# Second layer's attention: output products three tiles behind the scores instead of two

## The reference, cut to what matters

```python
def _L1_attn_ref(x, w_q_a, q_a_ln_w, w_q_b, w_kv_a, kv_a_ln_w, w_kv_b, w_o):
    ...
    q_full = jnp.concatenate([q_abs, q_pe], axis=-1)              # (b, s, 16, 128)
    k_full = jnp.concatenate([ckv, k_pe[:, :, 0, :]], axis=-1)    # (b, s, 128)
    scores = jnp.einsum('bqhd,bkd->bhqk', q_full, k_full) * sm_scale
    causal = jnp.tril(jnp.ones((s, s), dtype=bool))
    scores = jnp.where(causal[None, None], scores, jnp.finfo(scores.dtype).min)
    attn = jax.nn.softmax(scores, axis=-1)
    o_ckv = jnp.einsum('bhqk,bkr->bqhr', attn, ckv)
    y = jnp.einsum('bqhr,hre->bqe', o_ckv, w_o_abs)
    return y
```

## Time and profile before

| | us |
|---|---|
| median of 3 runs | 2657.73 |
| lowest and highest of them | 2649.23, 2659.24 |
| the profiled execution, whole | 2649.07 |
| its span, first to last instruction | 2647.1 |
| PE busy in the span | 2142.4 (81%) |
| ACT busy | 1163.7 (44%) |
| POOL busy | 699.5 (26%) |
| DVE busy | 1307.3 (49%) |

### The profile page before, as it was taken

One profiled execution on the slowest core, in us unless ns is written; L12 is line 12 of the kernel. 1 busy time (PEld: TensorE's weight loads), 2 busy tenths in 40 slices (PEclk: granted clock), 3 DMA queues, 4 the chain that ended last, 5 costly groups with the idle time before them and its releaser, 6 DMA issues. The chain is left out here.

```text
span 2647.1 us, 39558 instructions
## 1 busy us (share of the span) xinstructions
PE 2142.4 (81%) x10988; PEld 1373.2 (52%) x10988; DVE 1307.3 (49%) x2944; ACT 1163.7 (44%) x2316; POOL 699.5 (26%) x800
## 2 busy tenths in 40 slices
PE   5886899999872128999974579999978899997798
PEld 2542223333241114788864235777764577775587
DVE  5776778888127003344432566444425544442543
ACT  1663567777611001222211225777723477774222
POOL 1331000000010750000001663666620166663100
PEclk6786899999955557999987788999989899998899
DMA  7800000000101520777764320011000001102000
GB/s 221 254 1 1 1 0 0 0 0 0 36 1 30 180 78 8 214 224 223 225 178 125 88 81 15 21 30 30 21 25 0 3 21 30 29 22 76 0 17 16
DMA packets 186659, 167.16 MB, mean 63 GB/s; under 512 B 18787, under 2 KB 172949, under 8 KB 186326
## 3 DMA queue, kind: packets, MB, share of 16 engines
q1 hardware_dynamic: 175510, 139.42, 18.3%
q0 software_dynamic: 9696, 26.75, 3.1%
q10 hardware_dynamic: 1376, 0.02, 0.0%
HBM read 96.15 MB, written 61.60 MB: 60 GB/s over the span
## 5 line engine op out<-in xcount | busy, mean ns | idle before, releaser
L2404 POOL TENSOR_TENSOR w_rest<-work,w_head 128x512 fp32r<-128x512 f32 (+3 forms) x384 | 395.5, 1036 | 294.6 <-ACT w_head L2361 274.4
L725 DVE TENSOR_REDUCE half_max<-m_ps 128x1 f32<-128x512 f32 x512 | 319.5, 684 | 69.3 <-PE m_ps L645 67.8
L2266 DVE TENSOR_REDUCE piece_max<-m_ps 128x1 f32<-128x512 f32 (+3 forms) x384 | 201.6, 553 | 279.8 <-PE m_ps L2191 211.3
L782 ACT ACTIVATE weights<-s_ps 128x512 f32<-128x512 f32 x512 | 264.7, 606 | 69.9 <-PE s_ps L664 69.3
L2357 ACT ACTIVATE work<-s_ps 128x512 f32<-128x512 f32 (+3 forms) x384 | 187.9, 489 | 145.6 <-PE s_ps L2218 85.6
L645 PE MATMUL m_ps<-kT,qT 96*128 (+1 forms) x512 | 210.7, 413 | 13.8 <-ACT weights L782 5.5
L664 PE MATMUL s_ps<-qT,kT 99*128 (+1 forms) x512 | 193.9, 389 | 20.8 <-ACT weights L782 20.3
L2361 ACT ACTIVATE w_head<-work 128x512 fp32r<-128x512 f32 (+3 forms) x384 | 201.5, 525 | 12.2
L2227 PE MATMUL o_ps<-w_head,lat_head 128*128 128x512 f32 (+3 forms) x384 | 171.4, 446 | 15.3 <-POOL w_rest L2404 15.3
L974 PE MATMUL ex_up_ps<-rowsT,ex_wgv 128*128 128x256 f32 (+1 forms) x768 | 177.9, 382 | 2.3 <-DMA ex_wo<-in_L_ffn_wo_dram 1.4
L974 PEld LDWEIGHTS ex_up_ps<-rowsT,ex_wgv 128*128 128x128 f32 (+1 forms) x768 | 143.5, 187 | 25.6 <-DMA ex_wo<-in_L_ffn_wo_dram 1.8
(11 more groups left out here) (363 smaller groups left out, 4262.5 us busy)
## 6 DMA issues: line engine op xcount, KB each, us to landing
slots<-zero SPq DMA_DIRECT2D x8, 3456.0 KB, 27.4
rows<-slots SPq DMA_DIRECT2D x64, 256.0 KB, 2.8
slots<-ex_out SPq DMA_DIRECT2D x64, 256.0 KB, 2.1
ex_wgv<-in_L_ffn_wg_dram SPq DMA_DIRECT2D x76, 176.0 KB, 2.7
ex_wgv<-in_L_ffn_wv_dram SPq DMA_DIRECT2D x76, 176.0 KB, 3.2
ex_wo<-in_L_ffn_wo_dram SPq DMA_DIRECT2D x76, 128.0 KB, 3.1
oT<-work SPq DMA_DIRECT2D x64, 128.0 KB
w_down<-l_inverse SPq DMA_DIRECT2D x32, 256.0 KB, 3.8
```

What stands on the lines that cost most here:

```text
L725: dve.tensor_reduce(half_max[:, u // 16, u // 2 % 8, u % 2:u % 2 + 1], m_ps[:, BANK[u], :], AX.X, ALU.max).then_inc(max_done, 1)
L782: act.activation(w[:, s % 2 * 4 + j, :], s_ps[:, BANK[4 * s + j], :], ACT.Exp, scale=HD ** -0.5).then_inc(w_done, 1)
L2266: dve.tensor_reduce(piece_max[:, qt, k0 // 512:k0 // 512 + 1], m_ps[:, r % 2, 0:n], AX.X, ALU.max).then_inc(d["max_done"], 1)
L2404: pool.tensor_tensor(w_rest[:, s % 3, c0:512], w[:, s % 3, c0:512], w_head[:, s % 3, c0:512], ALU.subtract).then_inc(d["w_rest_done"], 1)
```

## The change

`LAG` goes from 2 to 3. PE issues the outputs of a tile behind the scores of the third tile after it; the outputs of tiles 9, 10 and 11 now come in the next head, or, for the last head, behind its last scores. DVE's two evacuations move one row maximum later, to stand again behind the outputs that they wait for. The buffers, their numbers and all waits on semaphores stay as they are.

```diff
-    LAG = 2
+    LAG = 3
...
-                        if behind and r == 3:
+                        if behind and r == 4:
                             evacuate(h - 1, 1)
-                        if r == 7:
+                        if r == 8:
                             evacuate(h, 0)
```

## The result

| | before | after |
|---|---|---|
| median, us | 2653.73 (6 runs) | 2627.76 (6 runs) |
| lowest and highest | 2648.61, 2659.24 | 2622.87, 2635.25 |
| profiled execution | 2649.07 | 2627.17 |
| its span | 2647.1 | 2625.2 |

The ratio is 0.9915 with a 95% interval of 0.9898 to 0.9933: the change makes the kernel 0.85% faster, some 22 us. Forecast were 19 us, and a time of 2638 in 2627 to 2650.

A forecast was written before the change was run, and what follows sets the result against it. PE was taken to bound the attention, waiting for w_rest at table loads. 12 x 1.25 = 15.0 us plus 4.0 in the last heads, seams zero, gave 19.0 off the median 2657.73: 2638 us, range 2627 to 2650.

The forecast's parts named there:

- What bounds the kernel: Second layer's attention: PE is the bound; twelve waits for POOL's w_rest ahead of a head's first outputs cost 1.25 us each.
- PE's arrival: At tile 0' outputs: PE arrives at 1711.49 after the change, against 1711.32 when the outputs could begin before.
- the chain on ACT: w_head of tile 11 waits for tile 8's outputs, ending 1706.43; it began at 1706.45 anyway, so timing holds within some 0.05 us.
- The forecast margin: At tile 0' outputs: w_rest is ready 0.12 to 0.17 us before PE arrives, so the whole wait goes.
- The cover: On ACT, place_shift (1.02 us) hides w_head of tile 11's new wait; without it the cost is up to 0.81 us.
- My slower rival: w_head holds back ACT's next exponential, so PE waits at tile 3' scores in every head; 2671 us; chance 0.04.
- DVE at nothing: DVE's evacuations (0.69 us each) move with their outputs; the row maximum behind has 1.3 us, so cost is nothing.
- The last heads: Each batch's last head: four waits, 0.67, 0.56, 0.24 and 0.22 us, go; worth 1.69 to 2.73, taken as 2.0, twice.
- Seams: Narrow blocks get other neighbours on PE: 0.09 us a seam, 2.9 us either way over 32 heads, taken as zero.
- The wait that is only shortened: Tile 8's outputs reach ACT's chain, 0.66 us of each of 12 waits stay; gain 11, 2647 us; chance 0.12.
- The collision of POOL and DVE: A 0.68 us query rest falls ahead of tile 0's w_rest; 0.53 us stay twelve times; 2645 us; chance 0.03.
- the change does nothing: The wait at a head's first outputs hangs on the free slot, not ACT; time stays 2657 us; chance 0.03.

The follow-up runs named there:

- without loads: Changed kernel (lag 3) with ACT's loop over pairs written out, so no table loads between heads: ratio 0.9915 to the kernel before, stretches 309.90 and 309.74 us.
- The padded kernel: Changed kernel (lag 3) plus one 512-column ACT copy into a spare tile behind every head's last tile: ratio 0.9949 to the kernel before.
- Lag 4: Changed kernel with LAG 4 instead of 3, same three slots, evacuations behind maxima 5 and 9: ratio 1.0048 to the kernel before, stretches 327.14 and 327.74 us.
- lag 2 without loads: Kernel before (lag 2) with ACT's loop over pairs written out, so no table loads between heads: ratio 0.9940, stretches 312.38 and 312.96 us.

## Why the prediction was right, point by point

**What bounds the kernel.** PE did, and each wait removed was time won. A loaded head fell from 20.51 to 19.26, by the 1.25 us that the periods had given, twelve times: 15.0 us as forecast (0.05 of the 1.25 is what the other heads gained too). A pair takes 38.47 us, where 38.5 was forecast.

**PE's arrival and the chain on ACT.** The sum put the outputs of tile 0' 11.49 - 4.57 = 6.92 us behind the turn of the maxima (1704.57). In the trace after they come 1707.30 - 1700.48 = 6.82 behind it. The forecast margin of 0.12 to 0.17 us was mis-sized: `w_rest` of tile 0' began at 1705.96 and takes 1.27, so it ended at 1707.23, 6.75 behind the turn. PE wanted it at almost the same moment: in heads without a load it reaches this block 6.79 us behind the turn. Two terms made the difference. On ACT, `w_head` of tile 11 began 0.05 us later behind the turn than before, as the sum had allowed, and everything behind it followed. On PE, the sum took 0.24 us from the row product to the outputs, but the outputs come 0.07 behind it where nothing holds them, here in the kernel before in a head without a load:

```profile
1690.68 0.39 PE L2188 MATMUL m_ps<-k_head,qT 128*128 128x512 bf16 x1
1690.75 0.56 PE L2227 MATMUL o_ps<-w_head,lat_head 128*128 128x512 f32 x1
```

That is 0.17 us less than the sum had; with 0.04 more in the other blocks PE is there at 6.79 and not 6.92, and the margin was no more than that. Loaded heads keep 0.05 us that the others don't (19.26 against 19.21, and 19.21 everywhere without loads). The padded kernel says the same, since its first 0.5 us are paid in full. That the 1.25 us went in full is luck in this sense: any 0.1 us more on ACT's chain would have come off the gain twelvefold.

**The cover.** That `place_shift` hides the new wait of `w_head` was right with lag 3: it began 1.93 us behind the turn (1702.41 less 1700.48) against 1.88 before. Lag 4 shows what the term is worth when the held `w_head` stands ahead of `place_shift`, not behind it: 1.0 us in every head. My slower rival had the kind right, ACT's queue held up by `w_head`, but named the exponential and tile 3' as the point where it decides. The `w_head` of tile 10, which stands ahead of `place_shift`, comes first, and I had not looked at it for lag 3 either.

**DVE at nothing.** Right, but only because the diff moves the evacuations as well; with the old places it is 0.8 us a head. At its old place the evacuation of tiles 0 to 3 holds up maximum 8, whose slot PE wants one block of scores behind the outputs that the evacuation waits for. At its new place it holds up maximum 9, whose slot PE wants another block of outputs and of scores later.

**The last heads.** 2.0 us each were forecast, and the last column shows 1.92, in the changed kernel and without loads. But the agreement is luck: with lag 3 PE has issued one 512-wide block of outputs less by the last maximum of each head, so that block is missing in the first head's time and is added to the last. It shows in the first head. From the row product behind the scores of its tile 2 to the next mark it takes 11.22 and 11.21 us before, 10.51 and 10.51 after. So the waits of a last head cost 1.92 + 0.70 = 2.6 us, near the upper end of the 1.69 to 2.73 and not the lower. The two short gaps cost a restart as well. Of the four waits one is left, on the last outputs:

```profile
1931.12 0.33 PE L2227 MATMUL o_ps<-w_head,lat_head 128*128 128x128 f32 x1 [0.16 <-POOL w_rest L2404]
```

**Seams.** Taken at zero within 2.9 us: the unloaded heads are 0.05 us shorter, some 0.7 us in both batches. The sign was open and the size is a quarter of the bound. That these are seams is not shown: no wait is listed in these heads with either lag, and the blocks' times differ by up to 0.1 us in both directions.

**The rest of the gain.** 15.0 from the loaded heads, 0.7 from the others and 5.2 from the last heads are 20.9 us, against the stretches' 20.65. What is left is the start of the first heads, behind a pause of PE, at a granted clock below full (0.59 in the 10 us from batch 1's first mark before, 0.62 after). From the first mark to that row product they take 7.19 and 8.12 us before and 7.73 and 7.92 after, 0.3 us more in all. This varies from run to run whatever the lag: 7.41 and 8.13 in the changed kernel again, 7.35 and 7.92 with lag 2 without loads.

**The time.** Against the median the gain came out larger than the forecast (26 us between medians, 22 by the ratio of the runs), because the medians scatter by some us. The median of the kernel before came down from 2657.73 over three runs to 2653.73 over six, so that the forecast of 2638 stood 4 us too high from the start; the stretches give 1.65 us more than the 19.0, and 1.3 us lie outside the stage. 2627.76 is inside the range by less than 1 us. The low end was there for such scatter, but that it held is luck.

**The rivals.** The wait that is only shortened did not come, but it is what the pad makes of the kernel. The collision of POOL and DVE did not show: in a loaded head DVE's query rest began at 1703.99 and took 0.68 us, so it ended 1.3 us before the `w_rest` of tile 0' began at 1705.96; heads without a load take 19.21 us with `normalise` in them and without. That the change does nothing was refuted by the trace at once.

## What to carry to other kernels

When one engine is the bound and a wait shows at one place of a loop only, compare periods of turns with and without it before believing the bracket (here 1.25 us against 0.99), and ask what the late engine did there that it doesn't do elsewhere; here a hardware loop on ACT reloaded its table at each turn. A longer distance between two steps over the same ring of slots does not lengthen the time that the ring allows from freeing a slot to needing it again. It only moves the wait to the step that refills a slot, so look at what is queued behind that refill on its engine (here `place_shift` and `query_head`), and move every consumer of the delayed result by the same amount.

## What the runs showed that I had not expected

- An extra 0.6 us on ACT, 16 times a batch, costs lag 3 6.0 us and lag 2 12.8: at equal work, what counts is how many heads have no margin, 12 with lag 3 and all of them with lag 2.
- Leaving two short copies on VectorE, 0.69 us each, one place too early costs as much (0.85%) as the whole change brings.
- The whole kernel before differs by 4% between chips (2555 and 2650 us), while a head of this attention without a load takes 19.26 us with lag 2 at both levels.
